# A two-layer decoder on one core: VectorE's long chain pieces cut into several steps of the plan, with maxima between them

## The chip, the cores and the metric

One Trainium2 chip, of which the kernel uses one core. Its engines run side by side, each through its own fixed list of instructions: TensorE (PE for matmuls, PEld for the loads of weights), VectorE (DVE), ScalarE (ACT), GpSimd (POOL) and SyncE (SP, which here issues all the DMAs). They meet at semaphores only. The metric is the time of the program on the device in microseconds (us), the median of several runs.

## What is computed

Eight sequences of 256 tokens by 128 features go through two decoder layers, six residual parts in all:

```
x = x + linear_attention(layernorm(x))               # "phase 0": 16 heads, causal
x = x + cross_attention(layernorm(x), ctx, mask)     # phase 1: 16 heads, 512 keys
x = x + experts(layernorm(x))                        # 8 experts, the 2 best, gates renormalised
x = x + windowed_attention(layernorm(x))             # phase 2: 16 heads, causal, window of 128
x = x + cross_block(layernorm(x), ctx)               # phase 3: 8 heads, 512 keys, with two
                                                     #   layernorms and a feed-forward inside
x = x + ternary_ffn(x)                               # ternary weights, rms norms
```

The gates of the experts are `softmax(x @ Wg + bg)`, cut to the two largest and divided by their sum. The softmax of phases 1 to 3 needs a row maximum for each query and head.

## The kernel before

**Two kinds of work.** The *cores* of the attention phases (scores, maxima, exponentials, weighted values) are cut into uniform units. The *chains* are all the rest: for every sequence b a run "to0" (into phase 0), "to1", "to2" (which holds the experts too), "to3" and "end". Three lanes carry one run each at a time. A chain is a long line of short dependent steps that goes from engine to engine: DVE takes the statistics of a layernorm, POOL makes the root and the normed rows (L701, L695, L707), PE turns them (L821), ACT copies them out, PE multiplies, ACT and DVE and POOL split queries and keys into three bf16 parts each, SP spreads the parts into DRAM (L594) and, when all have landed, loads them back stacked (L633, L634).

**The maxima.** A unit of a maximum is one PE matmul into one of two PSUM banks `mb` (L985; for phase 2 L981 and L982) and one DVE reduction of that bank (L1451 in phase 1, L1454 and L1455 in phase 2, L1459 in phase 3). PE waits before unit n until DVE has taken unit n-2 (`pe.wait_ge(max_used, e.n + 1)`), so PE can be two units ahead of DVE and no more. After a group of four heads a "turn" brings the maxima through POOL (L798 to L802), PE (L973), DVE (L1446) and SP (L654) into rows of the scores' matmul.

**The order of everything.** Nothing is decided while the kernel runs. A planner written in Python gives each unit a time in planned microseconds, and each run of a chain a start. A step of a chain says with `yield t` when it is due, in local units of its run; the planned time is start + 1.5 t, and for t past `SLOT_AT` (44.0 for "to2", 20 for "to1" and "to3", 8.5 for "to0") also plus `held`, the time that the run waits for a free slot of the attention's buffers. `weave` then merges the maxima, the exponentials and the three lanes by planned time, and each engine gets its instructions in that order. What stands between two `yield`s is one piece that nothing is put into. The planned times of the units are 1.2 (phases 1 and 2) or 1.1 (phase 3) planned microseconds apart. All units and runs together take 929 to 931 planned microseconds.

**VectorE's pieces that the change touches.**

- `stats_of` (L1244, L1247): `bn_stats` for two blocks of 128 tokens, a wait for their end (`link`), then `bn_aggr` for both, which POOL's root waits for. It is called 64 times: in each `take`, in `experts` and three times in "end".
- `split_queries` (L1253, L1254, L1256): second part of the queries, then the third. Called 32 times. SP spreads part 2 at local 9.4 and part 3 at 9.5 after the take's start, DVE's piece is due at 8.2.
- The gating in `experts`, from L1359 to L1378, once in each of the eight "to2" runs: a reciprocal, products, comparisons, the ranks, the two best gates and their renormalisation, as one piece due at 15.5. PE needs it at 20 (L888).
- The experts' sums (L1391): four pieces per run, due at 25 + 2.8 i, each of four dependent multiply-adds. PE puts the next experts' matmul into the same bank (L899, due at 24 + 2.8 i) after DVE has ended the piece: `pe.wait_ge(experts_used[l], n * 4 + (i + 1))`.

Of the kernel before, what the change touches and what calls it, by code (L numbers as in the profile page):

```python
# [381 lines left out]
def decoder(nc, x, ctxT, maskq, maskk, weights, columns, rows_in, experts_bias, out):  # L382
    with ExitStack() as ctx:
# [36 lines left out]
        X = sbs(B, "X", [P, TQ, D])  # L420
# [783 lines left out]
        def _(dve):  # L1204
# [35 lines left out]

            def stats_of(run, src):
                l = run.lane
                for t in range(TQ):
                    ins = V_.bn_stats(stats[l][:, t, :], src[:, t, :])  # L1244
                link(ins, plain=True)
                for t in range(TQ):
                    ins = V_.bn_aggr(mv[l][:, t, :], stats[l][:, t, :])  # L1247
                ins.then_inc(ln_stats[l], 1)

            def split_queries(run):  # L1250
                l, before = run.lane, N_TAKES(run) * PARTS
                dve.wait_ge(q_part[l], before + 1)
                link(V_.tensor_tensor(xs[l][:, 0:S], xs[l][:, 0:S], parts[l][:, 0, 0:S], ALU.subtract))  # L1253
                V_.tensor_copy(parts[l][:, 1, 0:S], xs[l][:, 0:S]).then_inc(q_part[l], 1)  # L1254
                dve.wait_ge(q_part[l], before + 2)
                V_.tensor_tensor(parts[l][:, 2, 0:S], xs[l][:, 0:S], parts[l][:, 1, 0:S], ALU.subtract).then_inc(q_part[l], 1)  # L1256
# [17 lines left out]
            def take(run, p, at, k):  # L1274
                l, b, slot = run.lane, run.b, run.new.slot
                yield at + 0.2
                if p == 0:
                    dve.wait_ge(x_in[b], 16)
                stats_of(run, X[b])
                if p == 0:  # L1280
                    yield 8.6
                    n = N_TO0(run)
                    dve.wait_ge(xs_act[l], n + 1)
                    link(V_.tensor_scalar(xs[l][:, 0:2 * S], xs[l][:, 0:2 * S], 0.0, None, ALU.max))
                    yield 9.5
                    values(run, p)
                    V_.scalar_tensor_tensor(xs[l][:, 0:2 * S], f32_scratch[l][:, 0:2 * S], 1.0, xs[l][:, 0:2 * S], ALU.min, ALU.add).then_inc(xs_ready[l], 1)
                    yield 12.0
                    dve.wait_ge(xs_ready[l], n + 1)
                    dve.wait_ge(qf_ready[l], n + 1)  # L1290
                    split_queries(run)
                    yield 14.5
                    dve.wait_ge(filled[l], fill(run, "kv"))
                    V_.tensor_tensor(KV[slot][:], side[:, l, :].rearrange("p (h e) -> p h e", h=16),
                                     own[:].unsqueeze(2).to_broadcast([P, 16, VW]), ALU.mult).then_inc(lane_free[l], 1)
                else:
                    yield at + 8.2
                    split_queries(run)
                    yield at + 9.5
                    values(run, p)  # L1300
# [28 lines left out]
            def norm_affine(run, k, src, centred, g, dst, b_, at):  # L1329
                l = run.lane  # L1330
                yield at
                stats_of(run, src)
                dve.wait_ge(ln_stats[l], N_STATS(run) + k)
# [11 lines left out]
            def experts(run):  # L1345
                l, b, n = run.lane, run.b, N_TO2(run)
                bank = side[:, l, :]
                yield 6.2
                stats_of(run, X[b])
                yield 13  # L1350
# [8 lines left out]
                link(V_.reciprocal(grec[l][:], gsum[l][:]))  # L1359
                link(V_.tensor_tensor(gp[l][:], gp[l][:], grec[l][:].unsqueeze(2).to_broadcast([P, TQ, NE]), ALU.mult))  # L1360
                flat = gp[l][:].rearrange("p t e -> p (t e)")
                cmp_gt = xs[l][:, 2 * S:2 * S + P].rearrange("p (m j) -> p m j", j=NE)
                cmp_eq = xs[l][:, 2 * S + P:3 * S].rearrange("p (m j) -> p m j", j=NE)
                for t in range(TQ):
# [4 lines left out]
                    ins = V_.tensor_tensor(cmp_eq[:, sl, :], pj, pe_, ALU.is_equal)  # L1369
                link(ins)  # L1370
                eq = cmp_eq.rearrange("p (t e) j -> p t e j", t=TQ)
                link(V_.tensor_tensor(eq, eq, first[:].unsqueeze(1).to_broadcast([P, TQ, NE, NE]), ALU.mult))
                link(V_.tensor_tensor(cmp_gt, cmp_gt, cmp_eq, ALU.add))
                link(V_.tensor_reduce(rank[l][:].rearrange("p t e -> p (t e)"), cmp_gt, AX.X, ALU.add))
                link(V_.scalar_tensor_tensor(gate[l][:].rearrange("p t e -> p (t e)"), rank[l][:].rearrange("p t e -> p (t e)"), 2.0, flat, ALU.is_lt, ALU.mult))
                link(V_.tensor_reduce(gsum[l][:], gate[l][:], AX.X, ALU.add))
                link(V_.reciprocal(grec[l][:], gsum[l][:]))
# [7 lines left out]
                for i in range(4):  # L1385
                    t, half_ = i // 2, i % 2
                    yield 25 + 2.8 * i
                    dve.wait_ge(filled[l], fill(run, f"expert {i}"))
                    for e in range(4):
                        last = half_ == 1 and e == 3  # L1390
                        ins = V_.scalar_tensor_tensor((X[b] if last else acc)[:, t, :], bank[:, e * D:(e + 1) * D],  # L1391
# [9 lines left out]
            def chain_steps(run):  # L1401
# [12 lines left out]
                else:  # L1414
# [11 lines left out]
                    link(normed.pop())  # L1426
                    stats_of(run, X[b])
                    yield 39.7
# [112 lines left out]
```

## Time and profile before

| what | value |
|---|---|
| time, median of 3 runs (lowest, highest) | 1154.66 us (1147.33, 1155.74) |
| the profiled execution's own time | 1146.01 us |
| its span, first to last instruction | 1144.3 us |
| PE busy, DVE busy | 854.7 us (75%), 667.8 us (58%) |
| ACT busy, POOL busy | 459.3 us (40%), 383.1 us (33%) |
| mean granted TensorE clock | 0.906 |
| instructions | 19524 |

The profile is of one execution. "Busy" is the time in which at least one instruction of the engine runs. An idle stretch of an engine is put down to the instruction whose semaphore ended it. Matmuls overlap each other, so a start that follows the last one closely is no sign of a wait.

### The profile page before, as it was taken

The page shows a single profiled execution, that of the slowest core. Times are in us where ns is not written, and L with a number is a line of the kernel's source. Part 1 is how long each engine was busy: PE and PEld are TensorE (multiplying, and loading weights), DVE is VectorE, ACT ScalarE, POOL GpSimd, SP SyncE. Part 2 cuts the span into 40 slices and gives each one's busy share as a digit, 9 for nine tenths or more (in the row PEclk, how much of TensorE's full clock was granted, in tenths as well). Part 3 has the DMA queues.
Part 4 walks back from the last instruction along what each step waited for, and adds up shares of the span by engine and source line. Part 5 has one row for each costly group of instructions (what it writes and reads, how often), then busy time and mean ns, then how long its engine had stood idle before and what let it go on. Part 6 is the DMA issues. An engine that isn't in the chain of part 4 may idle for free.

```text
span 1144.3 us, 19524 instructions
## 1 busy us (share of the span) xinstructions
PE 854.7 (75%) x6459; PEld 481.8 (42%) x6522; DVE 667.8 (58%) x2234; ACT 459.3 (40%) x923; POOL 383.1 (33%) x872
## 2 busy tenths in 40 slices
PE   0466757988888887887787677888988777874666
PEld 0244544334333343444443455553534434651345
DVE  6646655667776764765677474376566484444431
ACT  0322213554444443544454222654645334651432
POOL 7524343210313222443223246433232125360033
PEclk9778978999999998999999888899999698995877
DMA  5357774031220204641233334543120602224100
GB/s 177 101 88 165 166 168 90 11 56 32 42 49 16 51 19 86 125 96 53 57 56 81 59 78 108 138 73 58 35 53 16 104 2 53 64 64 76 16 1 10
DMA packets 124964, 79.84 MB, mean 70 GB/s; under 512 B 8312, under 2 KB 122176, under 8 KB 124736
## 3 DMA queue, kind: packets, MB, share of 16 engines
q1 hardware_dynamic: 124864, 78.59, 33.2%
q8 instruction: 52, 0.85, 0.3%
q14 instruction: 48, 0.39, 0.1%
HBM read 43.99 MB, written 32.90 MB: 67 GB/s over the span
## 4 chain that ended last, share of the span: by engine, by line
PE 42%; DVE 21%; issue 10%; POOL 10%; DMA 8%; SPq 4%; ACT 4%; another core or an unknown queue 1%; DVEq 0%; POOLq 0%; ACTq 0%
PE ob L1042 7%; PE mb L985 5%; POOL hn L707 4%; DMA KS<-bounce 4%; DVE junk L1451 3%; PE side L861 3%; PE eb L1012 3%; PE eb L1013 2%; DVE mx L1459 2%; DMA QW<-bounce 2%; PE side L916 2%; DVE An L1391 2%; PE side L899 2%; PE side L908 2%; POOL rstd L695 2%
## 5 line engine op out<-in xcount | busy, mean ns | idle before, releaser
L1183 ACT ACTIVATE probs<-eb 128x512 f32<-128x512 f32 (+1 forms) x512 | 287.5, 571 | 401.9 <-PE eb L1013 172.7
L1451 DVE CUSTOM_DVE_ANT_0 junk<-mb,maskq_add 128x512 bf16<-128x512 f32 x256 | 172.1, 690 | 110.1 <-PE mb L985 82.3
L798 POOL TENSOR_SCALAR nm<-mx 128x8 bf16<-128x8 f32 x80 | 20.7, 259 | 428.7 <-DVE mx L1451 193.4
L1042 PE MATMUL ob<-probs,V 128*32 128x256 f32 (+1 forms) x2048 | 138.3, 390 | 3.3 <-ACT probs L1183 2.1
L1459 DVE TENSOR_REDUCE mx<-mb 128x1 f32<-128x512 f32 x128 | 85.0, 687 | 75.8 <-PE mb L985 74.0
L1012 PE MATMUL eb<-maskk_add,identb 128*128 128x512 bf16 x256 | 99.9, 390 | 6.6 <-DMA QP<-mrow 2.7
L985 PE MATMUL mb<-KS,QP 128*128 128x512 bf16 x230 | 89.0, 394 | 13.0 <-DVE mx L1451 12.1
L1013 PE MATMUL eb<-QP,KS 128*128 128x512 bf16 x233 | 90.6, 389 | 0.0
L1042 PEld LDWEIGHTS ob<-probs,V 128*32 128x32 f32 x2048 | 55.4, 113 | 77.7 <-issue 46.3
L985 PE MATMUL mb<-KS,QW 112*128 112x512 bf16 x128 | 53.0, 432 | 36.0 <-DMA QW<-bounce 21.3
L1454 DVE CUSTOM_DVE_ANT_0 junk<-mb,winq_add 128x128 bf16<-128x128 f32 x128 | 37.1, 290 | 68.1 <-PE mb L982 66.4
L707 POOL TENSOR_SCALAR hn<-X,mv,rstd 128x128 f32<-128x128 f32 x80 | 72.2, 910 | 4.3
L821 PE MATMUL side<-ident,hn 128*128 128x128 f32 x80 | 18.8, 322 | 64.0 <-POOL hn L707 62.6
L1190 ACT COPY OT<-ob 128x512 f32<-128x512 f32 x56 | 32.7, 584 | 73.0 <-PE ob L1036 52.2
L1469 DVE TENSOR_TENSOR probs<-eb,tri 128x512 f32<-128x512 f32 x64 | 42.3, 685 | 32.8 <-PE eb L1002 31.4
L713 POOL TENSOR_TENSOR xs<-xs,scratch 128x256 f32<-128x256 f32 (+1 forms) x32 | 30.4, 950 | 92.5 <-ACT scratch L1118 57.0
L861 PE MATMUL side<-ident,OT 128*128 128x36 f32 (+1 forms) x448 | 55.7, 281 | 5.6 <-issue 5.3
L861 PEld LDWEIGHTS side<-ident,OT 128*128 128x128 f32 x448 | 55.6, 198 | 9.9 <-issue 8.3
L1016 PE MATMUL eb<-QW,KS 112*128 112x256 bf16 x256 | 50.3, 292 | 9.8 <-ACT probs L1183 3.4
L701 POOL TENSOR_SCALAR rstd<-mv 128x2 f32<-128x2 f32 x64 | 16.0, 250 | 120.1 <-DVE mv L1247 118.3
L985 PEld LDWEIGHTS mb<-KS,QP 128*128 128x128 bf16 x256 | 25.7, 101 | 68.4 <-DVE mx L1451 40.1
L1455 DVE CUSTOM_DVE_ANT_0 junk<-mb,winq_add 128x256 bf16<-128x256 f32 x128 | 53.8, 420 | 0.2 <-issue 0.2
(186 smaller groups left out, 1706.0 us busy)
## 6 DMA issues: line engine op xcount, KB each, us to landing
QP<-bounce SPq DMA_DIRECT2D x48, 256.0 KB, 5.6
KS<-bounce SPq DMA_DIRECT2D x32, 384.0 KB, 7.5
bounce<-scratch SPq DMA_DIRECT2D x48, 192.0 KB, 2.3
bounce<-scratch SPq DMA_DIRECT2D x64, 128.0 KB, 2.1
KS<-bounce SPq DMA_DIRECT2D x32, 192.0 KB, 5.9
bounce<-scratch SPq DMA_DIRECT2D x16, 384.0 KB, 2.6
cT<-ctxT_dram SPq DMA_DIRECT2D x16, 256.0 KB, 2.9
bounce<-scratch SPq DMA_DIRECT2D x16, 256.0 KB, 3.0
```

Of the source, the lines that this page charges most:

```text
L707: ins = G.tensor_scalar(dst[:, t, :], src[:, t, :], mv[l][:, t, 0:1], rstd[l][:, t:t + 1], ALU.subtract, ALU.mult)
L861: ins = nc.tensor.matmul(bank[:, lo:lo + 4 * n].rearrange("p (h e) -> p h e", e=n), OT[o][:, g, t * P:(t + 1) * P], chosen, start=True, st ...
L985: ins = nc.tensor.matmul(bank, q_of(core, h)[:, 0, t * P:(t + 1) * P], k_of(core, h, 0, SK), start=True, stop=True)
L1012: nc.tensor.matmul(part, identb[:], maskk_add[:, kt:kt + 1, :].to_broadcast([P, 2, S]), start=True, stop=False, skip_group_check=True)
L1013: ins = nc.tensor.matmul(part, k_of(core, h, kt * P, P), q_of(core, h, 2), start=False, stop=True, skip_group_check=True)
L1016: ins = nc.tensor.matmul(bank[:, j * S:(j + 1) * S], k_of(core, h + j, kt * P, P), q_of(core, h + j)[:, 0, :], start=True, stop=True)
L1042: ins = nc.tensor.matmul(bank[32 * j:32 * j + 32, S - n:S], v_of(core, kt, 4 * g + j), pr[:, (j % 2) * n:(j % 2 + 1) * n], start=(kt == 0) ...
L1183: nc.scalar.activation(probs[:, u % PROBS, 0:n], eb[:, u % 2, 0:n], ACT.Exp, scale=SCALE[core.p]).then_inc(probs_by[1], 1)
L1451: ins = V_.tensor_tensor_reduce(junk[:, e.n % 2, :], bank, maskq_add[:, t, :], 1.0, NEG_EXP, ALU.add, ALU.max, mx[slot][:, t, h:h + 1])
L1455: ins = V_.tensor_tensor_reduce(junk[:, e.n % 2, P:3 * P], bank[:, P:3 * P], winq_add[:, 1:3, :].rearrange("p a k -> p (a k)"), 1.0, NEG_E ...
L1459: ins = V_.tensor_reduce(mx[slot][:, t, h:h + 1], bank, AX.X, ALU.max)
L1469: V_.tensor_tensor(probs[:, u % PROBS, :].rearrange("p (j q) -> p j q", j=4), eb[:, u % 2, :].rearrange("p (j q) -> p j q", j=4), tri[:].u ...
```

## The change

Inside the long pieces there are new `yield`s, so that the plan may put other work between their parts. No instruction, no wait and no data is changed, and PE's, ACT's, POOL's and SP's lists stay as they are; only the order of VectorE's list differs. The due times are written by hand:

- statistics: the aggregation 0.6 after the stats (`at + 0.8` in a take);
- query splits: the third part 0.6 after the second;
- gating: five parts at 15.5, 16.3, 17.1, 17.9 and 18.7;
- experts' sums: two products at 25 + 2.8 i, two at 25.9 + 2.8 i.

```diff
-            def stats_of(run, src):
+            def stats_of(run, src, at_):
...
                 link(ins, plain=True)
+                yield at_ + 0.6
                 for t in range(TQ):
                     ins = V_.bn_aggr(mv[l][:, t, :], stats[l][:, t, :])
...
-            def split_queries(run):
+            def split_queries(run, at_):
...
                 V_.tensor_copy(parts[l][:, 1, 0:S], xs[l][:, 0:S]).then_inc(q_part[l], 1)
+                yield at_ + 0.6
                 dve.wait_ge(q_part[l], before + 2)
...
-                stats_of(run, X[b])
+                yield from stats_of(run, X[b], at + 0.2)
...
-                    split_queries(run)
+                    yield from split_queries(run, 12.0)
...
-                    split_queries(run)
+                    yield from split_queries(run, at + 8.2)
...
                 link(V_.tensor_tensor(gp[l][:], gp[l][:], grec[l][:].unsqueeze(2).to_broadcast([P, TQ, NE]), ALU.mult))
+                yield 16.3
...
                 link(ins)
+                yield 17.1
...
                 link(V_.tensor_tensor(cmp_gt, cmp_gt, cmp_eq, ALU.add))
+                yield 17.9
...
+                yield 18.7
                 link(V_.tensor_reduce(gsum[l][:], gate[l][:], AX.X, ALU.add))
...
                     for e in range(4):
+                        if e == 2:
+                            yield 25.9 + 2.8 * i
...
                     link(normed.pop())
-                    stats_of(run, X[b])
+                    yield from stats_of(run, X[b], 23.6)
```

`norm_affine` and the statistics at 6.2 in `experts` are changed in the same way.

## Rows read from the trace of the kernel before

**Rows 1.** The page: span, busy time of two engines, chain that ended last.

```profile
span 1144.3 us, 19524 instructions
...
PE 854.7 (75%) x6459; PEld 481.8 (42%) x6522; DVE 667.8 (58%) x2234; ACT 459.3 (40%) x923; POOL 383.1 (33%) x872
...
PE 42%; DVE 21%; issue 10%; POOL 10%; DMA 8%; SPq 4%; ACT 4%; another core or an unknown queue 1%; DVEq 0%; POOLq 0%; ACTq 0%
```

**Rows 2.** Waits of PE: who waited for whom, us in total, times, longest.

```profile
PE side L821 <- POOL hn L707: 62.6, 20, 27.3
...
PE mb L985 <- DVE mx L1459: 12.2, 23, 2.2
...
PE side L899 <- DVE An L1391: 3.6, 4, 1.4
...
PE mb L985 <- DVE mx L1455: 0.2, 1, 0.2
```

**Rows 3.** Groups by line of DVE: count, busy us, mean ns, idle before.

```profile
L1451 DVE CUSTOM_DVE_ANT_0 junk<-mb,maskq_add 128x512 bf16<-128x512 f32 x256 | 172.1, 690 | 110.1 <-PE mb L985 82.3 <-remote 24.3 <-DVE An L1391 0.9
...
L1391 DVE SCALAR_TENSOR_TENSOR An<-side,gate,An 128x128 f32<-128x128 f32 x112 | 39.0, 349 | 7.1 <-PE side L899 4.2
...
L1244 DVE BATCH_NORM_STATS2 stats<-X 128x6 f32<-128x128 f32 x96 | 23.0, 282 | 1.0
```

**Rows 4.** Timeline round the gating: start, us, instruction [idle before, releaser].

```profile
257.01 0.14 DVE L1359 RECIPROCAL grec<-gsum 128x2 f32<-128x2 f32 x1
...
259.65 0.18 DVE L1378 TENSOR_TENSOR gate<-gate,grec 128x16 f32<-128x16 f32 x1
259.77 0.69 DVE L1451 CUSTOM_DVE_ANT_0 junk<-mb,maskq_add 128x512 bf16<-128x512 f32 x1
...
260.75 0.38 PE L1012 MATMUL eb<-maskk_add,identb 128*128 128x512 bf16 x1 [1.59 <-DVE mx L1451]
...
847.73 0.57 PE L985 MATMUL mb<-KS,QW 112*128 112x512 bf16 x1 [2.18 <-DVE mx L1459]
```

**Rows 5.** Timeline of PE, first and last stall behind a residual with statistics.

```profile
291.17 0.39 PE L985 MATMUL mb<-KS,QP 128*128 128x512 bf16 x1 [1.77 <-DVE mx L1451]
...
787.35 0.28 PE L973 MATMUL mb<-identb,nm 128*12 128x128 bf16 x2 [1.55 <-DVE mx L1451]
```

**Rows 6.** Timeline, first and last handover of experts' sums from DVE to PE.

```profile
272.16 1.51 DVE L1391 SCALAR_TENSOR_TENSOR An<-side,gate,An 128x128 f32<-128x128 f32 x4
...
273.72 1.12 PE L899 MATMUL side<-W,hT 128*128 128x512 f32 x2 [0.60 <-DVE An L1391]
...
929.01 1.50 DVE L1391 SCALAR_TENSOR_TENSOR An<-side,gate,An 128x128 f32<-128x128 f32 x4
...
931.39 0.23 PE L981 MATMUL mb<-KS,QP 128*128 128x128 bf16 x1 [1.44 <-DVE mx L1459]
...
931.57 1.02 PE L899 MATMUL side<-W,hT 128*128 128x512 f32 x2
```

**Rows 7.** Timeline of POOL: three runs' statistics at once.

```profile
58.05 0.23 POOL L701 TENSOR_SCALAR rstd<-mv 128x2 f32<-128x2 f32 x1 [8.46 <-DVE mv L1247]
```

**Rows 8.** Timeline round 1010 us: another lane's step follows the aggregation.

```profile
1010.47 0.58 DVE L1340 SCALAR_TENSOR_TENSOR X<-hn,rstd,X 128x128 f32<-128x128 f32 x2
...
1010.65 0.23 POOL L701 TENSOR_SCALAR rstd<-mv 128x2 f32<-128x2 f32 x1 [3.13 <-DVE mv L1247]
```

**Rows 9.** Timeline of POOL: normed rows at the start, beside DVE's copies, and later.

```profile
16.91 10.28 POOL L707 TENSOR_SCALAR hn<-X,mv,rstd 128x128 f32<-128x128 f32 x2
...
28.30 1.58 POOL L707 TENSOR_SCALAR hn<-X,mv,rstd 128x128 f32<-128x128 f32 x2
```

**Rows 10.** Timeline: spreading of a "to2" run's parts, DVE's place, and the first maximum.

```profile
372.78 2.02 SPq L594 DMA_DIRECT2D bounce<-scratch  x4
...
375.76 0.69 DVE L1451 CUSTOM_DVE_ANT_0 junk<-mb,maskq_add 128x512 bf16<-128x512 f32 x1
...
406.96 0.29 DVE L1454 CUSTOM_DVE_ANT_0 junk<-mb,winq_add 128x128 bf16<-128x128 f32 x1 [0.82 <-PE mb L982]
```

More of the change, by code:

```diff
@@ L1331, in norm_affine @@
                 yield at
-                stats_of(run, src)
+                yield from stats_of(run, src, at)
                 dve.wait_ge(ln_stats[l], N_STATS(run) + k)
@@ L1348, in experts @@
                 yield 6.2
-                stats_of(run, X[b])
+                yield from stats_of(run, X[b], 6.2)
                 yield 13
@@ L1426, in chain_steps @@
                     link(normed.pop())
-                    stats_of(run, X[b])
+                    yield from stats_of(run, X[b], 23.6)
                     yield 39.7
```

## The prediction, made before the change was timed

> **What bounds the kernel now.** I read the page first. PE is busy 854.7 of 1144.3 us and DVE 667.8, and the chain that ended last lies on PE for 42% and on DVE for 21%, with POOL, DMA and issue making up most of the rest [rows 1]. So no engine is full. PE goes through one fixed list, and the time is what that list needs plus every place at which it stands still. The reader should see that a change that adds no instruction can only act through these stops.
>
> Next the waits of PE. The dearest is the turning of normed rows, 62.6 us in 20 waits for POOL, of which 27.3 us is the start; so chain latency costs PE more than anything that DVE does. Waits of a PE instruction for a row maximum are eleven rows of that view, from 12.2 us down to 0.2 us, and add to 54.6 us. That is the ceiling for a change that only brings maxima forward: 4.8% of the span. Waits for the experts' sums are 3.6 us in 4 waits [rows 2].
>
> Then the groups by line, for prices: a maximum takes 0.69 us (about 0.65 in a row, since they overlap a little), one multiply-add of an expert 0.35 us, one `bn_stats` 0.28 us [rows 3]. Last the timelines round each kind of piece, to see which PE stops lie behind them and how much time passes before the piece's result is used.
>
> **Where the new steps take effect.** I counted from the plan's times what falls between the parts. Gating: one maximum at each new `yield` in seven of the eight runs, none in the eighth. Experts' sums: at least one maximum in 26 of 32. Statistics: a maximum in 30 of 64, other lanes' pieces in 18 more, nothing in 16. Splits outside "to2": a maximum in 11 of 24. In "to2" the third part was due at 43.7 and is now due at 44.3, past `SLOT_AT` = 44.0, so `held` is added too: 3 to 22 maxima come between in six runs.
>
> **Gating, the gain.** The piece runs from 257.01 to 259.83, 2.8 us. PE uses up its two banks and stands 1.59 us until the maximum at 259.77 is through; in another run it stands 2.18 us [rows 4]. In all, seven of the eight gatings, some with a neighbour lane's split right behind them, have such a stop, 10.3 us together. Afterwards the longest part is the first, about 1.0 us, and a maximum follows each. PE produces a maximum each 1.3 us or so and DVE then needs 0.65 us plus a part of 0.5 to 1.0 us, so the two banks cover it. Between 0 (no stop is won back) and 10.3 us I take 8, near the upper end, since the parts are well below the two units of cover. The four maxima delay the gates by 4 x 0.65 = 2.6 us. That costs nothing: seven or eight maxima still lay between the end of the gating and PE's next need of it in all but the last run, where nothing is put in. Without that cover it would be 8 x 2.6 = 21 us.
>
> **Residual, statistics and last expert, the gain.** Where a residual and statistics stand together, often behind an expert's sum, PE stands until the next maximum is through: eight stops, 1.77 us the first and 1.55 us the last, 9.0 us in all [rows 5]. Now the maximum goes before the aggregation, and the expert's sum is halved. One maximum earlier by the aggregation and half an expert (0.70 us) [rows 3] in about half of them: I take 4 us, from 1 to 9.
>
> **Experts' sums, both signs.** Four multiply-adds take 1.5 us. PE's next matmul into the bank follows in 24 of the 32 pieces, and it follows closely: 0.05 to 0.06 us after the end in five, 0.5 to 0.7 us in three, 0.9 to 3.0 us in sixteen; the first (273.72 after 273.67) and the last (931.57 after 930.51) stand in the rows [rows 6]. In the last, PE had waited 1.44 us for the maximum behind the piece. That kind of stop adds to 5.1 us; with the maximum in the middle it is reached 0.70 us earlier, so I take back 2.5 us of it (0 to 5.1). Against it the sum ends later by one maximum and its 0.17 us of start, 0.86 us in all. In the five tight handovers PE waits that longer, in the three others about 0.3 us: 5 x 0.86 + 3 x 0.3 = 5.2 us. For the sixteen loose ones I take 0: there the maximum that stood between piece and matmul is just the one that moved. The upper bound is all 24 at 0.86 us, 20.6 us. Queued behind the waiting matmul on PE are the scores of the exponentials, so ACT waits too.
>
> **Statistics, the loss.** POOL waits for the aggregation and PE for POOL, so a delay is passed on where both are tight. (1) At 58.05 POOL had waited 8.46 us for the statistics of the first of three runs that start together [rows 7]. The order becomes stats, stats, stats, aggregation; two pairs of `bn_stats` more, at most 4 x 0.28 = 1.1 us, by their overlap 1.0 us. (2) The same at the very start: 1.0 us. (3) At 1010.65 POOL had waited 3.13 us, and behind the aggregation DVE had another lane's step of 0.58 us and its own pair of stats; these now come first: 1.1 us, on the path to the stack loads of a "to3" run that PE then waits for [rows 8]. (4) Five more places (near 340, 394, 625, 845 and 880 us), where a maximum or half an expert comes between and PE's turn followed POOL within 0.5 us: 0.2 to 0.9 us each, 2.8 us together. Sum 5.9 us, from 3 (some absorbed) to 8.
>
> At the start DVE's large copies run next. The normed rows there took 10.28 us for two instructions, later 1.58 us [rows 9]. The Trainium skill (SBUF — State Buffer, on engine ports and DMA ports) says that VectorE in its two-port modes and GpSimd lock one shared pair of ports for a whole instruction, whoever comes first. By that rule, with which this trace's 10.28 us agrees, POOL's root too would fall behind the copies and one normed block would still be left when they end, 1.5 us later in place of my 1.0 us; the loss would be 6.4 us and not 5.9.
>
> **Splits.** In "to2" run 1 SP spread four parts from 372.78; DVE comes to the new place of the third part only at 375.76, so SP waits, and its stack load is about 3 us later. The slot's first maximum is at 406.96 [rows 10], so 24 us of cover hide it. SP's later loads of turned maxima wait for DVE's still later places anyway. In the other runs the stack load waited for a buffer longer than that, or the delay is under 1.5 us. Cost 0; if the cover were gone, 3.1 us. The other splits: 0, bounds -1 to +2.
>
> **The sum.** -8 - 4 - 2.5 + 5.2 + 5.9 = -3.4 us: span 1144.3 to 1140.9. The profiled execution took 1146.01 us of its own, 8.65 us below the median of the runs, so I carry the difference over to the median: 1154.66 - 3.4 = 1151.3, call it 1151.
>
> **The rivals.**
>
> *A, faster by over 1%.* All stops behind maxima near these pieces go, 10.3 + 9.0 + 5.1 = 24.4 us, and the losses are the low 3 us of the statistics plus 5.2 us: -16.2 us, 1138.5. For it speaks that DVE's backlog behind a long piece also delays POOL's part of the turn. Against it: PE's next stops are often for DMA or POOL, and a gain before such a stop is lost there.
>
> *B, slower.* One mechanism: the handover of the experts' bank. PE may be two maxima ahead of DVE, but the second half of a sum is due only 0.9 local, 1.35 planned us, so little more than one maximum, ahead of PE's matmul. If most of the 24 handovers become tight, the loss is 20.6 us in place of 5.2, and with only 5 us of the other gains kept the sum is -5 + 20.6 + 5.9 = +21.5; with all of my gains it is +12.0, 1166.7. From about eighteen tight handovers on (18 x 0.86 = 15.5, sum +6.9) it decides the sign clearly. Speaks for it: five have 0.06 us to spare already. Against: in the loose ones PE itself was held back by the maximum that moves.
>
> *C, no net effect.* The stops at maxima are won back and spent at the next stop in PE's list, above all the turns behind POOL (62.6 us) [rows 2], and the losses are likewise absorbed: 0 us, 1154.7.
>
> **How the numbers follow.** The forecast (about -3, with its own range of -9 to +4: 1146 to 1159) has 0.40, C 0.15, A 0.24, B 0.21. The range reaches to the middle of A and of B: low 1137, high 1168. A measurement of this kernel can tell about 1% from no change (1143 and 1166 are the bounds). Faster by over 1%: A, 0.24. Within 1%: the forecast and C, 0.55. Slower: B, 0.21.
>
> **What would show it.** Right: no PE stop over 0.6 us behind a gating; waits of PE for maxima down from 54.6 to about 40 us; waits of L899 for L1391 up from 3.6 to about 9 us; POOL's aggregation at the second start 1.0 us later; DVE's busy time unchanged. Wrong: L899's waits at 20 us (then B), or waits for maxima down by 20 us with the time down by as much (A). If PE's waits fall and DMA or POOL waits grow by the same, it is C. My prediction would be wrong if the order of VectorE's list moved something that I took as covered, such as the third part of the queries.

## The result, and the profile after

The changed kernel takes 1169.5 us (median of 4 runs, 1161.99 to 1174.86) where the kernel before took 1152.66 us beside it: a ratio of 1.0146, 95% interval 1.0112 to 1.0179, so 16.8 us slower. In a second comparison it took 1166.02 us (6 runs), ratio 1.0127 (1.0094 to 1.016). The prediction was 1151.0 us, with a range of 1137 to 1168: the sign was wrong, and the first median lies outside the range. Executions over 1.5% above the fastest of their kernel are left out of every ratio here (two of e5's ten, with which its median would be 7.2 us above the kernel before in place of 5.0, one of e12's twelve, and two of the kernel before in the comparison of e15 and e16).

The page of the kernel after answers to [rows 1]; the line PEclk is the granted TensorE clock in 40 slices, in tenths:

```profile
span 1165.1 us, 19539 instructions
...
PE 873.3 (75%) x6459; PEld 488.2 (42%) x6522; DVE 661.0 (57%) x2234; ACT 460.0 (39%) x923; POOL 384.9 (33%) x872
...
PEclk9879978999999989898979878999999699886877
...
PE 41%; DVE 19%; POOL 12%; DMA 10%; issue 9%; SPq 4%; ACT 4%; DVEq 0%; another core or an unknown queue 0%; POOLq 0%; ACTq 0%
```

As many DVE instructions as before, and DVE is busy for 6.8 us less (the prediction had it unchanged; why is left open). PE, whose list is unchanged, is busy for 18.6 us more, with 6459 matmul records in both profiles, and idle for 2.2 us more. On the chain that ended last DVE has 2 points less and POOL and DMA 2 more each. The waits of the kernel after (who waited for whom, us in total, times, longest) answer to [rows 2]:

```profile
POOL rstd L701 <- DVE mv L1248: 155.9, 33, 13.1
...
PE side L821 <- POOL hn L707: 68.0, 23, 28.3
...
PE mb L985 <- DVE mx L1459: 12.7, 24, 1.1
PE side L899 <- DVE An L1399: 12.6, 14, 1.8
...
PE side L899 <- DVE X L1399: 3.7, 5, 0.9
```

(Lines moved down: L1399 is the experts' sums, L1248 the aggregation, L1459, L1463 and L1467 the maxima of phases 1, 2 and 3.) The part that the change was to improve did improve: all waits of PE for maxima add to 42.3 us, before 54.6. Against it stand the waits of L899 for DVE, 18.2 us with a small row for L1388 (before 5.3), and 5.4 us more behind POOL's normed rows. POOL's root waits 155.9 us for the aggregation; in the kernel before, the same row of the waits read

```profile
POOL rstd L701 <- DVE mv L1247: 118.3, 28, 10.5
```

The gating did as hoped. PE's timeline of the kernel after (start, us, instruction [idle before, releaser]) has two small stops where [rows 4] has one of 1.59 us, and the 2.18 us of the other run became 0.80 (the prediction had named 0.6 as the most that would be left):

```profile
262.56 0.39 PE L985 MATMUL mb<-KS,QP 128*128 128x512 bf16 x1 [0.58 <-DVE mx L1459]
263.85 0.39 PE L985 MATMUL mb<-KS,QP 128*128 128x512 bf16 x1 [0.46 <-DVE mx L1459]
...
865.54 0.39 PE L985 MATMUL mb<-KS,QW 112*128 112x512 bf16 x1 [0.80 <-DVE mx L1467]
```

**Where the handovers went.** One of the sixteen "loose" handovers, first in the kernel before:

```profile
327.74 1.12 DVE L1391 SCALAR_TENSOR_TENSOR An<-side,gate,An 128x128 f32<-128x128 f32 x3
...
328.89 0.35 DVE L1391 SCALAR_TENSOR_TENSOR X<-side,gate,An 128x128 f32<-128x128 f32 x1
328.95 0.59 PE L985 MATMUL mb<-KS,QP 128*128 128x512 bf16 x2
...
329.46 0.69 DVE L1451 CUSTOM_DVE_ANT_0 junk<-mb,maskq_add 128x512 bf16<-128x512 f32 x1 [0.22 <-PE mb L985]
...
330.44 1.02 PE L899 MATMUL side<-W,hT 128*128 128x512 f32 x2
```

and the same one in the kernel after:

```profile
332.76 0.73 DVE L1399 SCALAR_TENSOR_TENSOR An<-side,gate,An 128x128 f32<-128x128 f32 x2
...
333.97 0.59 PE L985 MATMUL mb<-KS,QP 128*128 128x512 bf16 x2
...
334.48 0.69 DVE L1459 CUSTOM_DVE_ANT_0 junk<-mb,maskq_add 128x512 bf16<-128x512 f32 x1 [0.99 <-PE mb L985]
...
335.10 0.69 DVE L1459 CUSTOM_DVE_ANT_0 junk<-mb,maskq_add 128x512 bf16<-128x512 f32 x1
...
335.71 0.34 DVE L1399 SCALAR_TENSOR_TENSOR An<-side,gate,An 128x128 f32<-128x128 f32 x1
336.09 0.35 DVE L1399 SCALAR_TENSOR_TENSOR X<-side,gate,An 128x128 f32<-128x128 f32 x1
...
336.50 0.70 PE L899 MATMUL side<-W,hT 128*128 128x512 f32 x1 [0.87 <-DVE X L1399]
```

The sum had everything it needed, but behind its first half DVE stands still for 0.99 us, for a maximum whose matmul PE has not made. From the first multiply-add to PE's next experts' matmul it was 2.70 us, now it is 3.74. Before, 5 of 24 handovers were tight (PE went on within 0.06 us of the sum's end); now 20 are.

**Where the aggregations went.** The same in an "end" run. DVE in the kernel before, then DVE and POOL in the kernel after:

```profile
899.53 0.49 DVE L1244 BATCH_NORM_STATS2 stats<-An 128x6 f32<-128x128 f32 x2
900.12 0.25 DVE L1247 BATCH_NORM_AGGREGATE mv<-stats 128x2 f32<-128x6 f32 x2
```

```profile
917.52 0.49 DVE L1244 BATCH_NORM_STATS2 stats<-An 128x6 f32<-128x128 f32 x2
924.45 0.69 DVE L1467 TENSOR_REDUCE mx<-mb 128x1 f32<-128x512 f32 x1 [6.44 <-PE mb L985]
925.06 0.24 DVE L1248 BATCH_NORM_AGGREGATE mv<-stats 128x2 f32<-128x6 f32 x2
...
925.39 0.38 POOL L701 TENSOR_SCALAR rstd<-mv 128x2 f32<-128x2 f32 x1 [10.84 <-DVE mv L1248]
```

The aggregation was due one maximum later. That maximum itself takes 0.69 us, but its matmul comes 6.44 us late, and 0.24 us of ready work waits all that time behind it. In the profile of the statistics cut alone (e3) DVE was idle between `bn_stats` and aggregation for 39 us in all (6.6 us in the kernel before), 30 us of it at nine of the 64 calls. (The Trainium skill, TensorE: Matmul & The Clock Gate, on the array's structure and the engines' queues, calls VectorE's queue strictly first in, first out; the trace agrees: 6.44 us of standstill and nothing passes.)

### The profile page after: what moved, and what is told of

The parts are those of the page before. It is cut to its first block, busy times and chain, and to the rows that moved or that the text cites. A ratio compares the mean times of both kernels' runs of the same rounds, so it can differ in the third digit from the quotient of the medians.

```text
span 1165.1 us, 19539 instructions
## 1 busy us (share of the span) xinstructions
PE 873.3 (75%) x6459; PEld 488.2 (42%) x6522; DVE 661.0 (57%) x2234; ACT 460.0 (39%) x923; POOL 384.9 (33%) x872
## 4 chain that ended last, share of the span: by engine, by line
PE 41%; DVE 19%; POOL 12%; DMA 10%; issue 9%; SPq 4%; ACT 4%; DVEq 0%; another core or an unknown queue 0%; POOLq 0%; ACTq 0%
PE ob L1042 7%; DMA KS<-bounce 5%; PE mb L985 5%; POOL hn L707 4%; PE side L861 3%; DVE junk L1459 3%; PE side L899 3%; PE eb L1012 3%; POOL rstd L695 2%; DVE mx L1467 2%; DMA QW<-bounce 2%; PE eb L1013 2%; DVE An L1399 2%; PE side L916 2%; PE side L908 2%
## 5 line engine op out<-in xcount | busy, mean ns | idle before, releaser
L1459 DVE CUSTOM_DVE_ANT_0 junk<-mb,maskq_add 128x512 bf16<-128x512 f32 x256 | 173.2, 689 | 124.2 <-PE mb L985 95.5
L1042 PE MATMUL ob<-probs,V 128*32 128x256 f32 (+1 forms) x2048 | 143.0, 401 | 2.0 <-ACT probs L1183 0.8
L1467 DVE TENSOR_REDUCE mx<-mb 128x1 f32<-128x512 f32 x128 | 85.6, 688 | 72.8 <-PE mb L985 69.3
L821 PE MATMUL side<-ident,hn 128*128 128x128 f32 x80 | 19.8, 335 | 68.2 <-POOL hn L707 68.0
L701 POOL TENSOR_SCALAR rstd<-mv 128x2 f32<-128x2 f32 x64 | 18.4, 287 | 157.3 <-DVE mv L1248 155.9
L707 POOL TENSOR_SCALAR hn<-X,mv,rstd 128x128 f32<-128x128 f32 x80 | 66.3, 836 | 4.3
L861 PE MATMUL side<-ident,OT 128*128 128x36 f32 (+1 forms) x448 | 58.3, 288 | 5.6 <-issue 5.1
L861 PEld LDWEIGHTS side<-ident,OT 128*128 128x128 f32 x448 | 58.1, 205 | 10.3 <-issue 8.8
L1463 DVE CUSTOM_DVE_ANT_0 junk<-mb,winq_add 128x256 bf16<-128x256 f32 x128 | 53.7, 419 | 0.2 <-issue 0.2
```

What stands on the lines that cost most here:

```text
L707: ins = G.tensor_scalar(dst[:, t, :], src[:, t, :], mv[l][:, t, 0:1], rstd[l][:, t:t + 1], ALU.subtract, ALU.mult)
L861: ins = nc.tensor.matmul(bank[:, lo:lo + 4 * n].rearrange("p (h e) -> p h e", e=n), OT[o][:, g, t * P:(t + 1) * P], chosen, start=True, st ...
L1042: ins = nc.tensor.matmul(bank[32 * j:32 * j + 32, S - n:S], v_of(core, kt, 4 * g + j), pr[:, (j % 2) * n:(j % 2 + 1) * n], start=(kt == 0) ...
L1459: ins = V_.tensor_tensor_reduce(junk[:, e.n % 2, :], bank, maskq_add[:, t, :], 1.0, NEG_EXP, ALU.add, ALU.max, mx[slot][:, t, h:h + 1])
L1463: ins = V_.tensor_tensor_reduce(junk[:, e.n % 2, P:3 * P], bank[:, P:3 * P], winq_add[:, 1:3, :].rearrange("p a k -> p (a k)"), 1.0, NEG_E ...
L1467: ins = V_.tensor_reduce(mx[slot][:, t, h:h + 1], bank, AX.X, ALU.max)
```

## The experiments

All make part of the change, on the kernel before. "us" is the ratio less 1, times 1152. The other columns are of one profiled execution each: waits of PE for maxima, of L899 for DVE, of L821 for POOL's hn, of POOL's L701 for the aggregation (all from the waits), and the mean granted clock. The profiles of before, after, e12, e13 and e14 hold 6459 of PE's matmuls, the others 6522, so sums of PE's busy time and of its waits are compared most safely within each group.

| run | ratio (95% interval) | us | maxima | L899 | L821 | L701 | clock |
|---|---|---|---|---|---|---|---|
| before | | | 54.6 | 5.3 | 62.6 | 118.3 | 0.906 |
| c1 before, again | 1.0000 (0.9976, 1.0024) | 0 | 52.8 | 4.9 | 62.6 | 118.8 | 0.905 |
| e1 gating | 0.9983 (0.9961, 1.0005) | -2.0 | 46.7 | 4.9 | 62.7 | 118.9 | 0.895 |
| e2 experts' sums | 1.0053 (1.0028, 1.0078) | +6.1 | 45.4 | 17.7 | 64.0 | 117.9 | 0.900 |
| e3 statistics | 1.0093 (1.0068, 1.0117) | +10.7 | 52.5 | 4.9 | 67.3 | 155.5 | 0.892 |
| e4 splits | 0.9958 (0.9935, 0.9982) | -4.8 | 48.3 | 5.2 | 62.6 | 118.0 | 0.900 |
| e5 all but statistics | 1.0043 (1.0012, 1.0073) | +5.0 | 38.9 | 17.8 | 63.2 | 115.3 | 0.907 |
| e6 gating, splits | 0.9970 (0.9949, 0.9991) | -3.5 | 47.1 | 5.2 | 61.5 | 118.0 | 0.905 |
| e7 all but sums | 1.0049 (1.0027, 1.0072) | +5.6 | 45.3 | 5.2 | 67.1 | 152.0 | 0.898 |
| e8 statistics, 55 calls | 1.0013 (0.9991, 1.0036) | +1.5 | 49.4 | 4.9 | 66.7 | 127.6 | 0.905 |
| e9 statistics, the other 9 | 1.0062 (1.0040, 1.0083) | +7.1 | 51.3 | 4.9 | 63.9 | 139.8 | 0.903 |
| e10 one call of the 9 | 1.0020 (0.9995, 1.0045) | +2.3 | 49.9 | 4.9 | 63.6 | 120.8 | 0.906 |
| e15 four of the 9 | 1.0024 (1.0007, 1.0042) | +2.8 | 51.7 | 4.7 | 63.4 | 131.9 | 0.899 |
| e16 five of the 9 | 1.0035 (1.0018, 1.0053) | +4.0 | 53.7 | 4.7 | 63.9 | 130.3 | 0.894 |
| e11 sums, halves further apart | 1.0164 (1.0129, 1.0198) | +18.9 | 44.6 | 29.1 | 63.3 | 118.9 | 0.903 |
| e12 whole without both causes | 0.9969 (0.9946, 0.9993) | -3.6 | 43.9 | 5.5 | 66.4 | 128.3 | 0.905 |
| e13 gating, splits, last sum | 0.9940 (0.9906, 0.9974) | -6.9 | 44.6 | 5.6 | 64.1 | 114.9 | 0.910 |
| after | 1.0146 (1.0112, 1.0179) | +16.8 | 42.3 | 18.2 | 68.0 | 155.9 | 0.896 |
| e14 after, again | 1.0127 (1.0094, 1.0160) | +14.6 | 39.2 | 18.2 | 66.6 | 154.5 | 0.895 |

**Each part alone.** In each kernel only the `yield`s of one part are kept:

```diff
+                yield 16.3            # e1: with 17.1, 17.9 and 18.7
+                            yield 25.9 + 2.8 * i      # e2
+                yield at_ + 0.6       # e3: in stats_of
+                yield at_ + 0.6       # e4: in split_queries
```

> Only the four new steps inside the gating; all else as in the kernel before. Theory H (the handover of the experts' bank makes the loss): no handover is touched, so the stops of PE behind the seven gatings go and the time falls by 5 to 8 us, ratio 0.993 to 0.996. Theory S (the later aggregation of the statistics makes it): the same, 5 to 8 us faster. Theory R (any re-ordering of VectorE's list costs, by the clock that TensorE is granted): no gain or 3 to 5 us slower, ratio 1.000 to 1.005, with more low-clock time than in the kernel before. Waits of PE for maxima 54.7 to about 45 us in all three.

> Only the experts' sums in two halves. Theory H: the waits of L899 for the sums rise from 5.3 us to about 17 us and the time with them by 10 to 17 us, ratio 1.009 to 1.015, most of the whole change's 1.0146. Theory S: at most 3 us slower, ratio 0.999 to 1.003, although the L899 waits rise. Theory R: 4 to 5 us slower, a quarter of the whole.

> Only the aggregation of the statistics as a step of its own. Theory S: 8 to 14 us slower, ratio 1.007 to 1.012, waits of L821 for POOL up by 5 us or more. Theory H: the start alone costs 2 to 3 us (aggregation of the first of three runs 1.0 to 1.2 us later, twice) and the rest another 0 to 3, ratio 1.002 to 1.005. Theory R: 4 to 5 us slower.

> Only the third part of the queries as a step of its own. Theories H and S: no difference, ratio 0.997 to 1.003, since the stack loads are covered. Theory R: 4 to 5 us slower. A fourth reading, that the third part (moved past the held time of the to2 runs) delays SyncE's queue on the path: 3 to 10 us slower, and the first maxima of phase 2 later by as much.

Two parts cost, statistics +10.7 and sums +6.1 us, and two gain. So the sign was not lost to the handovers of the sums alone. The statistics, meant to bring maxima forward too, brought none: PE's waits for maxima are 52.5 us as before.

**Pairs and triples.**

> The kernel before, unchanged, for a second profile. Its first one (1146.0 us) is near the fastest of its own runs (1145.0 to 1157.4). If the clock makes the spread, this one has more low-clock time than the 214.6 us of the first whenever it is slower, about 1.0 us of low clock for 0.4 to 0.6 us of time, and the same maxima at which all four single edits fell 4 us behind (between 490 and 530 us) fall behind here too. If it is not the clock, low-clock time is the same within 5 us at any time. Ratio 0.997 to 1.003 in either case.

> The whole change with the statistics in one piece again. If the four edits add up: -2.0 + 6.1 - 4.8 = -0.7 us, ratio 0.999. If the statistics and the sums hinder each other (the whole is 16.8 us, the four singles add to 9.9), the 7 us between them are in one of the pairs: with the statistics out and the 7 us in a pair of the others, ratio 1.005 or more; with them in a pair with the statistics, ratio 0.997 to 1.001.

> The two edits that did no harm alone. If they add up: -6.8 us, ratio 0.994 (0.992 to 0.997), faster than either kernel. If both win back the same stops (the gating of one run and the split of its neighbour stand back to back), no more than the better of the two, ratio 0.996.

> The whole change with the experts' sums in one piece again. If the four edits add up: -2.0 + 10.7 - 4.8 = +3.9 us, ratio 1.003. If the 7 us that the whole has over the sum of its edits lie in the pair of statistics and sums, the same 1.003; if they lie in a pair of the statistics with gating or splits, 1.007 to 1.010.

Gating and splits together gain 3.5 us, less than the 6.8 us of their two alone, though the intervals leave room: the gating of one lane often has a neighbour's split right behind it, and both win back one stop. PE's waits for maxima say the same: 6.1 and 4.5 us less for each alone, 5.7 us less for both together (against c1). With that pair taken as one, -3.5 + 6.1 + 10.7 = +13.3 us, and the whole had +16.8 and +14.6: the parts add, within the error. e7 lies below its sum (7.2) and e5 above its own (2.6), by about 2 us each, which is one interval.

**Which of the statistics.** The calls are told apart by the run's name, its sequence and the number of the call in it:

```diff
+            CUT = {("to1", 5, 1), ("to2", 4, 1), ("to2", 4, 2), ("to2", 5, 1), ("end", 1, 1),
+                   ("end", 1, 2), ("end", 3, 1), ("end", 5, 1), ("end", 5, 2)}
...
+                cut = (*key, CALLS[key]) not in CUT   # e8; e9: in CUT
...
-                yield at_ + 0.6
+                if cut:
+                    yield at_ + 0.6
```

> As the statistics alone, but nine of the 64 calls stay in one piece: those where, in the trace of that kernel, DVE had ended bn_stats and then stood idle for over 1 us at a maximum (or another lane's step) whose input PE had not made yet, with the aggregation queued behind it (near 194, 444, 512, 577, 680, 705, 916, 995 and 1024 us, idle 3.54, 1.95, 4.90, 6.24, 1.16, 1.14, 7.49, 2.88, 0.97 us). Theory 1, the loss is the aggregation held back behind a maximum that has no input yet: of the 10.7 us only the two starts (2.0 us) and a few tenths are left, 2 to 4 us over the kernel before, so about 1153. Rival, each cut costs the one maximum put in (about 0.65 to 0.9 us wherever PE or POOL is tight), wherever it stands: most of the 10.7 us stays, 8 to 10 us over, about 1160. A third reading, that the loss is mainly time at TensorE's lower clock level which the order brings by chance: between the two, with PE's busy time high and its idle time as before.

> The opposite of the run before: only the nine calls are cut. Theory 1: nearly the whole loss but the starts, 6 to 9 us over the kernel before, about 1158; POOL's waits for the aggregation up by some 25 us, and DVE idle between bn_stats and the aggregation for about 28 us over the nine. Rival (one maximum each): 9 x 0.86 = 7.7 us at most if all nine were tight, but they are nine of 30 with a maximum in between, so a share of 0.3, 2 to 3 us, about 1153.

> One call alone is cut, that of run to2 of sequence 4 before its phase 2; in VectorE's whole list the aggregation and one maximum change places, nothing else. In the trace of the statistics alone DVE waits 4.90 us there for the maximum's matmul, and the maxima behind it are 4.1 us later after it than before it. Theory 1: this one swap costs 3 to 5 us, about 1154.5. Rival (one maximum each): at most 0.9 us, no change that can be measured. The clock as the cause: no change of more than its scatter, and no step of the maxima at this place.

55 cuts cost 1.5 us, nine cost 7.1. The intervals of e8 and e9 do not touch, and the rival (one maximum for each cut, wherever it stands) had them the other way round. e10 decides nothing: 2.3 us, interval -0.6 to +5.2 us. Its single swap reads in DVE's timeline as a standstill of 4.95 us with the aggregation behind it:

```profile
507.90 0.69 DVE L1460 CUSTOM_DVE_ANT_0 junk<-mb,maskq_add 128x512 bf16<-128x512 f32 x1 [4.95 <-PE mb L985]
508.52 0.08 DVE L1460 DVE_READ_ACCUMULATOR2_ANT mx<- 128x1 f32 x1
508.52 0.24 DVE L1255 BATCH_NORM_AGGREGATE mv<-stats 128x2 f32<-128x6 f32 x2
```

Then the nine were split in two:

```diff
+            CUT = {("to1", 5, 1), ("to2", 4, 1), ("to2", 4, 2), ("to2", 5, 1)}   # e15
+            CUT = {("end", 1, 1), ("end", 1, 2), ("end", 3, 1), ("end", 5, 1), ("end", 5, 2)}   # e16
```

> Of the nine calls of the statistics only the four in runs to1 and to2 are cut (sequences 5, 4, 4, 5; near 194, 441, 505 and 571 us). With all nine cut DVE held these aggregations back for 0.95, 1.44, 4.98 and 5.73 us, 13.1 of 28.5 us. If the loss of the nine (7.1 us) follows the time held back, it is 3.3 us here. If it depends on who needs the result next: POOL's normed rows of these runs are turned by PE without a stop after three of the four, so 1 to 2 us.

> The other five, all in runs end (sequences 1, 1, 3, 5, 5; near 670, 697, 901, 979 and 1011 us; held back 2.64, 1.14, 7.80, 2.88 and 0.98 us, 15.4 of 28.5 us). There VectorE's own first step of the norm goes behind the aggregation too, and the feed-forward's chain follows. If the loss follows the time held back: 3.8 us. If it depends on who needs the result next: 5 to 6 us, since in the trace of the nine the maxima fall 3.3 us behind near 985 us and 2.5 us between 1005 and 1048 us, with a new stop of 1.29 us at L981 there.

2.8 and 4.0 us, which add to 6.8 beside the 7.1 of the nine, and lie near the 3.3 and 3.8 us of "it follows the time held back": about a quarter of a microsecond for each microsecond that the aggregation is held (13.2 and 14.4 us in these two profiles). The intervals, +-2 us, do not exclude that the place counts as well.

**Stops, or the clock?** The nine calls cost 7.1 us, but PE's stops do not show it: in the table e9 has 1.5 us less of waits for maxima than c1 and 1.3 us more behind POOL. The expectation of e8 had named a third reading, more time at TensorE's lower clock level. The granted clock has two levels here, 1.2 and 2.4 GHz, so 2 x (1 - mean clock) x span is the time at the lower one. The rows are differences of means over the 4 to 12 executions of each kernel to those of the kernel before beside it (21 to 34), in us; +- is a standard error, and half of the time at the lower level is an estimate of the most that it can cost:

| kernel | of the nine calls are cut | span | time at the lower level | half of that |
|---|---|---|---|---|
| e3 statistics | nine | +11.8 | +17.3 +- 4.5 | +8.6 |
| e9 the nine | nine | +6.7 | +12.1 +- 2.5 | +6.0 |
| e15 | four | +2.9 | +6.2 +- 1.8 | +3.1 |
| e16 | five | +4.5 | +11.6 +- 2.5 | +5.8 |
| e7 all but sums | nine | +5.3 | +10.8 +- 3.1 | +5.4 |
| e14 the whole | nine | +15.7 | +16.0 +- 4.8 | +8.0 |
| e8 the other 55 | none | +1.6 | -4.3 +- 3.0 | -2.2 |
| e2 sums | none | +5.5 | -0.3 +- 3.0 | -0.1 |
| e11 sums, further apart | none | +18.0 | +1.5 +- 3.9 | +0.8 |
| e12 without both causes | none | -2.8 | -6.1 +- 2.8 | -3.1 |

So the extra time at the lower level comes with the nine calls and goes with them, and it is large enough for most of what they cost. The sums cost without it. The profiles of c1 and of e3, with equally many matmul records, show where the time is:

```profile
span 1148.6 us, 19587 instructions
...
PE 865.6 (75%) x6522; PEld 480.3 (42%) x6522; DVE 667.2 (58%) x2234; ACT 459.4 (40%) x923; POOL 384.3 (33%) x872
```

```profile
span 1164.3 us, 19589 instructions
...
PE 880.8 (76%) x6522; PEld 489.1 (42%) x6522; DVE 665.4 (57%) x2234; ACT 459.6 (39%) x923; POOL 384.0 (33%) x872
```

PE is busy for 15.2 us more in e3 and idle for 0.5 us more. In e11 (span 1165.6 us, PE busy 869.7 us) it is the other way: 4.1 us more busy, 12.9 us more idle. How an aggregation that is held back brings the lower level about is not shown by any run here.

**The sums, with the suspected cause doubled.**

```diff
-                            yield 25.9 + 2.8 * i
+                            yield 26.5 + 2.8 * i
```

> The experts' sums alone cut, but the second half due at 26.5 + 2.8 i in place of 25.9, so that up to two maxima stand between the halves (twice the suspected cause). Theory, the handover of the bank to PE's next experts' matmul sets the loss: in the run with 25.9, 19 of the 24 handovers were tight (PE went on 0.05 to 0.06 us after the sum) and PE's waits at L899 for DVE were 17.7 us for +6.1 us; here nearly all are tight, these waits come to 30 us or more and the time to 12 to 18 us over the kernel before, about 1165. Rival, any cut of the sums costs the same whatever its place (start-up of an instruction, lost overlap): again about 6 us, 1156. Rival, the maxima that come earlier pay for it (PE waits less for them): below 6 us.

The waits of this kernel:

```profile
PE side L899 <- DVE An L1395: 18.4, 15, 2.7
...
PE side L899 <- DVE X L1395: 9.4, 7, 1.6
```

With two maxima in the middle, 22 of 24 handovers are tight and L899's waits are 29.1 us. The first rival (6 us again) and the second (less than 6) are out. The account of PE's waits closes within 3 us in both kernels. One maximum: 12.8 us more at L899 (over c1), 7.4 less for maxima, net 5.4, and the time is +6.1. Two: 24.2 more, 8.2 less, net 16.0, and the time is +18.9. So nearly all of the gain comes with the first maximum put in, the price with each.

**The whole without the two causes.**

```diff
-                        if e == 2:
+                        if e == 2 and i == 3:      # e12 and e13; e12 has the 55 calls as well
```

> The whole change, less its two suspected causes: the nine calls of the statistics stay in one piece, and of an expert's four sums only the last, which no matmul of PE waits for, is cut (8 of 32). Gating, splits, 55 of 64 statistics and 8 of 32 sums are cut as in the changed kernel. Theory 1, aggregations and sums held behind a maximum are the cause: the sum of the parts measured alone is -3.5 (gating and splits together) + 1.5 (statistics but nine) + 0 to -1 for the last sums, so -2 to -3 us, about 1149; waits of PE at L899 for DVE at 5 us, POOL's for the aggregation at 125 us. Rival, it is the number of cuts or the changed order as such (or the lower clock level that it brings): most of the 17 us stays, 1160 or more.

> Gating, splits and the last of the four sums of an expert run cut, statistics whole. Gating and splits alone were at 0.997 of the kernel before. If the cut of the last sum brings the maximum behind it forward and delays nothing that PE waits for, 0 to 2 us better than those two alone: 1145 to 1148. If the residual and the statistics that follow the last sum are on the path, it costs one maximum in some of eight places: 1149 to 1151.

> The changed kernel once more, beside the others on this chip. The parts measured alone add to -3.5 + 6.1 + 10.7 = +13.3 us; the whole had +16.8 in four runs, between 1162.0 and 1174.9. If the parts simply add, it lies at 1163 to 1167 in a larger number of runs; if the parts make each other worse, at 1168 or more. Its time at the lower clock level tells how much of that is the clock: 242 us in the first profile, 214 to 218 us in three executions of nearly or exactly the kernel before.

e12 has every cut of the change but 9 statistics and 24 sums, and it is 3.6 us faster than before. So these 33 cuts carry the whole loss; the number of cuts, or the new order as such, does not. Five handovers of the sums are tight in e12 and in e13, as in the kernel before. Measured in parts the 33 cost 16.6 us (7.1 for the nine, 9.5 for the sums without the 3.4 us that the last of them seem to gain, e13 against e6), and between e12 and the whole lie 18.2 to 20.4 us. e13 leaves all statistics whole and cuts only the sum that no matmul of PE waits for. At 1143.79 us it is the fastest kernel here, 0.6% below the one before (0.3 to 0.9%) and 2% below the changed one. The cores of c1, e13 and e14, in this order:

```profile
core 0: 1148.6 us, clock 0.905
```

```profile
core 0: 1137.4 us, clock 0.910
```

```profile
core 0: 1163.1 us, clock 0.895
```

## Why the prediction was wrong, by its own steps

Two steps failed: the 0 us for the sixteen loose handovers of the sums, and the price of a late aggregation, taken as the length of what is put before it. A premise failed with them, that the change "can only act through these stops" of PE: up to about half of the loss is time at the lower clock level, with PE busy.

**Gating, -8.** Waits for maxima fell by 6.1 us (e1 against c1), near my 8. The time fell by 2.0 us, interval -4.5 to +0.6. Mechanism right, size too large. That a stop won back is partly lost at PE's next stop for a DMA or POOL stood under A and C and not in the sum; it would explain the rest, but no run shows it.

**Residual, statistics and last expert, -4.** The term took one gain for two edits together, the later aggregation and the halved last sum. The statistics gave nothing (52.5 us for maxima, c1 52.8). The last sum's cut alone gave about 3.4 us (e13 against e6; their intervals overlap).

**Experts' sums, -2.5 and +5.2.** This step failed. The gain was more (-7.4), the loss much more (+12.8). The false sentence is "For the sixteen loose ones I take 0: there the maximum that stood between piece and matmul is just the one that moved." The maximum did move, but it took its own wait with it: it had stood idle for its matmul with the sum already complete, and now does so with half of the sum still to come. What I had as rival B (all 24 tight: 20.6 us) was the right mechanism at two thirds of its size, and 20 tight handovers passed the eighteen that I had named as deciding. By themselves the sums cost 6.1 us net.

**Statistics, +5.9.** This step failed too. I priced each delay by what is put before the aggregation, 0.65 us for a maximum, 1.0 us at each of the two starts. The starts came about as predicted: PE's first turn is 1.0 us later (28.31 against 27.34 us), and POOL's wait at the second start is 0.7 us longer than in [rows 7], 1.2 us longer with the statistics alone (e3, 9.63 us).

```profile
28.31 0.66 PE L821 MATMUL side<-ident,hn 128*128 128x128 f32 x2 [28.31 <-POOL hn L707]
...
60.60 0.23 POOL L701 TENSOR_SCALAR rstd<-mv 128x2 f32<-128x2 f32 x1 [9.17 <-DVE mv L1248]
```

(The Trainium skill's rule of the shared ports, SBUF — State Buffer, had POOL's root fall behind DVE's copies and the first turn come 1.5 us later. The trace agrees in kind: the root's two steps, 0.24 and 0.71 us long in the kernel before, take 2.38 and 4.73 us here, but the normed rows are then done in 3.79 us in place of 10.28. The size is not borne out; it is the 1.0 us worked out from the rows.)

```profile
17.08 2.38 POOL L701 TENSOR_SCALAR rstd<-mv 128x2 f32<-128x2 f32 x1 [3.96 <-DVE mv L1248]
19.55 4.73 POOL L695 TENSOR_TENSOR rstd<-rstd,constant 128x2 f32<-128x2 f32 x1
24.38 3.79 POOL L707 TENSOR_SCALAR hn<-X,mv,rstd 128x128 f32<-128x128 f32 x2
```

Term (3), 1.1 us at [rows 8], came too. POOL's wait there is shorter (2.85 us, before 3.13), but only because its wait began later. From the start of `bn_stats` to POOL's root it was 0.93 us, and now it is 2.16. First DVE's `bn_stats` before, to be read with [rows 8], then the kernel after:

```profile
1009.72 0.49 DVE L1244 BATCH_NORM_STATS2 stats<-X 128x6 f32<-128x128 f32 x2
```

```profile
1029.73 0.49 DVE L1244 BATCH_NORM_STATS2 stats<-X 128x6 f32<-128x128 f32 x2
1030.32 0.61 DVE L1342 SCALAR_TENSOR_TENSOR X<-hn,rstd,X 128x128 f32<-128x128 f32 x2
1030.96 0.49 DVE L1244 BATCH_NORM_STATS2 stats<-X 128x6 f32<-128x128 f32 x2
1031.55 0.38 DVE L1248 BATCH_NORM_AGGREGATE mv<-stats 128x2 f32<-128x6 f32 x4
...
1031.89 0.23 POOL L701 TENSOR_SCALAR rstd<-mv 128x2 f32<-128x2 f32 x1 [2.85 <-DVE mv L1248]
```

These delays are real, but the 55 calls that hold them cost 1.5 us together (-1.0 to +4.1), not 5.9. What I left out are the nine calls, 7.1 us. My count said which pieces get a maximum in between. It did not ask whether that maximum's input would be there.

**Splits, 0.** They gained 4.8 us, outside my bounds of -1 to +2: PE's waits for maxima fell by 4.5 us (e4 against c1). I had asked only what the later third part would delay, and not which stops lie behind a piece of 1.5 us (subtraction, copy and subtraction) that follows a gating.

**The sum.** With what the runs gave: -3.5 (gating and splits), +6.1, +10.7, in place of -8 + 0, -2.5 + 5.2 and -4 + 5.9. All three groups erred to the same side, by 4.5, 3.4 and 8.8 us, 16.7 in all. Rival B had the right sign, but for one cause where there were two. That its 1166.7 us lies so near the 1166 and 1169.5 us measured is luck: in it the sums cost 18.1 us and the statistics 5.9, measured 6.1 and 10.7.

**What the sum had no term for.** PE's list is the same, but it did not take the same time. From the profile of before to the two of after, with equally many matmul records, PE is busy 18.6 and 16.1 us more and idle 2.2 and 2.7 us more. A mean clock of 0.906 over 1144.3 us is 2 x 0.094 x 1144.3 = 215 us at the lower level, and 0.896 over 1165.1 us is 242 us. (The Trainium skill, TensorE: Matmul & The Clock Gate, in its terms, puts the penalty at half the time spent at the lower level; the profiles of c1 and e3 agree, with 33 us more at the lower level and PE busy 15.2 us more.) Single profiles mislead on the size, since the two of before lie at 0.906 and 0.905 where the mean of its executions is 0.900 to 0.902. Over the executions of the second comparison the whole spends 16.0 us more at the lower level, at most 8 of its 15.7 us by the estimate above, so up to about half. The lower level is no separate cause: e12, without the two causes, is back at 0.905. How the held aggregations bring it about isn't settled. PE's stops behind POOL do not explain the nine calls: with them alone L821 waits only 1.3 us longer than in c1, for 7.1 us of time.

## What to carry to other kernels

Before an instruction is put in front of ready work in an in-order queue, look at its own wait, not its duration: a row maximum of 0.69 us held 0.24 us of work back for up to 7.8 us, because its matmul had not been made. Cut a long piece where what follows the cut is needed by nobody soon (the gating, the splits, the last sum). Keep whole what another engine waits for (a bank that the next matmul fills, an aggregation) where the work put in between may itself have to wait. Counting the handovers without slack is not enough: 5 of 24 were tight before and 20 after, so loose ones are only loose while the order stands. And read the clock over many executions before a difference is put down to stops.

## What the runs showed of the hardware

The granted clock differs for the same work after nearly the same stop. Near 517 us of the kernel before PE stands for POOL's part of a turn (1.6 to 3.7 us in the nineteen profiles, in which this place lies between 512 and 532 us) and then does the same matmuls. The windows (PE busy, ..., granted clock in the last column but two) are of the kernel before and of e10, ten microseconds from that stop on:

```profile
516.80:526.80 10.00, 9.54 (x70) 6.76 (x72) 4.83 (x14) 4.69 (x11) 1.71 (x4) 1.00 0.34 111
```

```profile
516.60:526.60 10.00, 10.00 (x55) 6.73 (x54) 2.48 (x8) 2.56 (x6) 0.10 (x1) 0.66 0.06 20
```

and one matmul of 512 columns there, before and in e10:

```profile
519.86 0.38 PE L1012 MATMUL eb<-maskk_add,identb 128*128 128x512 bf16 x1
```

```profile
520.11 0.63 PE L1012 MATMUL eb<-maskk_add,identb 128*128 128x512 bf16 x1
```

The lower level is granted for part of this stretch in all seventeen profiles of a changed order (0.53 to 0.83 in such a window), also where little or nothing is changed near it (e1 and e4), and in neither of the two profiles of the kernel before. e1 and e4 are not slower for it. A step of a few us in one profile at such a place is therefore no evidence for the edit made there; I had first read e10's 5 us of lag behind this place as the price of its swap, and the median says 2.3.
